# Set-up, first preparation, gate and residual of a masked-attention and ternary-FFN kernel rearranged

## What is computed

```python
norm  = |xn|;  mean = mean of xn over the tokens
score = 0.7 * norm + 0.3 * (-(xn . mean) / (norm * |mean| + 1e-6))
lm    = the int(0.33 * 1024) tokens with the highest score   # landmarks
lm    = lm dilated twice by one token to both sides
mask  = (j <= i) & ((i - j < 128) | lm[j])
s     = softmax(q k^T / 4 + mask) v @ Wo          # 16 heads of 16, 8 k/v heads
w1q, w2q = sign(w) where |w| >= 0.7 * mean|w|, else 0
g     = silu(gelu(xn @ w1q^T + b1) @ w2q^T + b2)  # exact gelu, 1024 hidden
out   = x + s * g
```

## Time and profile before

| | us |
|---|---|
| median of 3 runs | 701.88 (701.42 to 702.69) |
| the profiled execution | 701.2 |
| its span, first to last instruction | 699.5 |
| set-up, to the last copy on ACT | 32.6 |
| first preparation, to turn 0's first matmul | 94.6 |
| PE busy | 581.8 |
| ACT busy | 459.1 |
| DVE busy | 399.2 |
| POOL busy | 260.1 |

### The profile page before, as it was taken

The page is one execution under the profiler, slowest core; times in us unless marked ns, Lnnn a source line. Parts: engine busy times, 40 slices in busy tenths (PEclk is TensorE's granted clock), DMA queues, the critical chain, the costliest instruction groups (busy, mean ns, idle before and its releaser), DMA issues. The chain is left out here.

```text
span 699.5 us, 10945 instructions
## 1 busy us (share of the span) xinstructions
PE 581.8 (83%) x3725; PEld 298.1 (43%) x3725; DVE 399.2 (57%) x957; ACT 459.1 (66%) x584; POOL 260.1 (37%) x303
## 2 busy tenths in 40 slices
PE   1559559889799979889799879889899899799973
PEld 1447315534353636534353635534353545323512
DVE  2757937848557548848557638948475644411111
ACT  4313747787578755787578756787678767797670
POOL 3313523422533433431533433431543353345431
PEclk9779859999999979999999969999999989899995
DMA  7001153202132252202132242102132233031101
GB/s 233 3 2 47 48 116 84 63 8 74 35 93 56 64 146 70 58 9 75 34 94 57 63 146 72 57 9 78 38 101 54 60 84 95 26 89 59 38 15 48
DMA packets 51227, 45.49 MB, mean 65 GB/s; under 512 B 9056, under 2 KB 45536, under 8 KB 51168
## 3 DMA queue, kind: packets, MB, share of 16 engines
q1 hardware_dynamic: 49040, 42.90, 22.1%
q10 hardware_dynamic: 2128, 1.84, 0.8%
HBM read 11.41 MB, written 4.19 MB: 22 GB/s over the span
## 5 line engine op out<-in xcount | busy, mean ns | idle before, releaser
L1575 ACT ACTIVATE f_probs<-sc_ps,shift 128x1024 f32<-128x1024 f32 (+3 forms) x384 | 332.9, 901 | 132.8 <-PE sc_ps L1475 127.5
L1475 PE MATMUL sc_ps<-f_q_stack,f_k_stack 104*128 104x512 bf16 (+3 forms) x768 | 200.3, 352 | 39.3 <-ACT f_probs L1575 22.5
L1492 PE MATMUL att_ps<-f_probs,f_v_sb 128*32 128x512 f32 (+3 forms) x1536 | 168.8, 514 | 12.2 <-POOL f_probs L1634 10.1
L1627 POOL TENSOR_SCALAR_AFFINE_SELECT f_probs<-f_probs 128x512 f32<-128x512 f32 x128 | 94.7, 741 | 131.2 <-ACT f_probs L1575 130.5
L1475 PEld LDWEIGHTS sc_ps<-f_q_stack,f_k_stack 104*128 104x128 bf16 x768 | 48.9, 100 | 205.4 <-ACT f_probs L1575 124.2
L1634 POOL TENSOR_TENSOR f_probs<-f_probs,f_near 128x512 f32<-128x512 f32 x64 | 75.0, 1172 | 110.7 <-ACT f_probs L1575 110.7
L1413 PE MATMUL aux_ps<-w2T,f_h_hi 128*128 128x256 f32 x256 | 72.5, 316 | 0.0
L1614 POOL TENSOR_TENSOR f_h_lo<-f_hid,f_h_hi 128x512 fp32r<-128x512 f32 x36 | 47.9, 1337 | 54.9 <-DVE f_h_hi L1687 47.1
L1492 PEld LDWEIGHTS att_ps<-f_probs,f_v_sb 128*32 128x32 f32 x1536 | 31.4, 110 | 77.4 <-issue 47.7
L1413 PE MATMUL aux_ps<-w2T,f_h_lo 128*128 128x256 f32 x256 | 63.4, 281 | 0.0
L1403 PE MATMUL aux_ps<-f_xT_hi,w1T 128*128 128x512 f32 x128 | 54.7, 427 | 6.8 <-ACT f_hid L1528 6.6
(11 more groups left out here) (174 smaller groups left out, 756.9 us busy)
## 6 DMA issues: line engine op xcount, KB each, us to landing
f_q_stack<-f_q_parts SPq DMA_DIRECT2D x192, 64.0 KB
f_k_stack<-f_k_parts SPq DMA_DIRECT2D x96, 64.0 KB, 2.6
xn<-in_L_attn_hidden_states SPq DMA_DIRECT2D x4, 1024.0 KB, 6.7
f_attT<-f_att_raw SPq DMA_DIRECT2D x128, 32.0 KB
f_rden_bc<-f_den SPq DMA_DIRECT2D x64, 64.0 KB
s_w_nat<-in_L_ffn_w SPq DMA_DIRECT2D x2, 1024.0 KB, 9.1
out_y<-xn SPq DMA_DIRECT2D x4, 512.0 KB, 3.2
xn<-in_L_attn_hidden_states SPq DMA_DIRECT2D x3, 512.0 KB, 3.9
```

The costliest lines, as they stand in the source:

```text
L1475: last = pe.matmul(sc_ps[:, 2 * u + hh, lo:CH], k_stack[0:KROWS + T, h // REP, kb * P:(kb + 1) * P], q_stack[0:KROWS + T, SLOT[n], 2 * u + ...
L1492: last = pe.matmul(att_ps[32 * q:32 * q + 32, n % 2, lo:CH], v_sb[:, kb, j * VW:j * VW + 32], probs[:, i % NPROB, q, lo:CH], start=(kb == ...
L1575: act.activation(probs[:, i % NPROB, us, lo:CH], sc_ps[:, us, lo:CH], ACT.Exp, bias=shift[:, 0:1], scale=HD ** -0.5).then_inc(exp_done, 1)
L1627: pool.affine_select(out=block_probs, in_=block_probs, compare_op=ALU.is_ge, fill=0.0, base=0, pattern=[[0, NQ], [1, P]], channel_multipli ...
```

## The change

1. Set-up. x is the first transfer on SP's queue, and ACT waits for it before it issues the four weight transfers. DVE finishes `rstd` and normalises x before the thresholds. PE sums the normalised x over the tokens (8 matmuls) behind the Gram matmuls; DVE copies the mean row and takes the eight token dots between links of the bound chain.
2. First preparation. Mean row, normalising and token dots are gone from it. Its jobs use six banks (two of `aux_ps`, four of `sc_ps`). The token scores come first on DVE, ranks are laid between the splits of k and q, which use `attT` for their rest, and the wait for the last q split is gone.
3. `rank(t)` takes three instructions: one counts `>=` over the earlier tokens, one `>` over its own and the later ones, one adds the equal ones of its own block that stand ahead.
4. The sum of x over the tokens in a turn is three additions of halves in place of one reduction.
5. silu(z) = z (1 + tanh(z/2)) / 2. ACT takes tanh at steps 15 and 44 between exponentials; DVE multiplies at steps C1 + 3 and 46; the factor 0.5 goes into the product of the output projection. `gates()` is gone.
6. The residual x has a tile `x_res` of its own, filled from step group 0 on, before `att_group(0)`.
7. POOL does the masks of a step before its jobs.
8. `fast_path()` stands in the `If` and `general_path()` in the `Else`.

```diff
@@ set_up @@
+                        sp.dma_start(xn[:, :, :], x[0].rearrange("(t p) d -> p t d", p=P)).then_inc(x_in, 16)
                         sp.dma_start(w1_nat[:, :, :], w1.rearrange("(t p) d -> p t d", p=P)).then_inc(w1_in, 16)
...
-                        act.dma_start(xn[:, :, :], x[0].rearrange("(t p) d -> p t d", p=P)).then_inc(x_in, 16)
+                        act.wait_ge(x_in, 16)
                         act.dma_start(w_nat[:, :, 0:D], Wq.rearrange("(k p) n -> p k n", p=P)).then_inc(wqkv_in, 16)
...
                             layer_norm(dve, lk, k)
+                        for _ in inverse_deviation(dve, lk):
+                            pass
+                        for k in range(T):
+                            dve.tensor_scalar(xn[:, k, :], xn[:, k, :], mv[:, k, 0:1], rstd[:, k:k + 1], ALU.subtract, ALU.mult).then_inc(x_normal, 1)
...
+                        def token_dots(t):
+                            for k in range(t, t + 2):
+                                dve.scalar_tensor_tensor(w_tmp[:, 0, (k - t) * D:(k - t + 1) * D], xn[:, k, :], 1.0, mean_row[:, :],
+                                                         ALU.mult, ALU.mult, accum_out=dots[:, k:k + 1]).then_inc(set_dots, 1)
+                            dve.wait_ge(set_dots, t + 2)
...
+                        dve.wait_ge(mean_sum_done, 1)
+                        dve.tensor_scalar(mean_row[:, :], att_ps[:, 0, 0:D], 1.0 / S, None, ALU.mult).then_inc(mean_out, 1)
...
+                        for t in range(T):
+                            pe.wait_ge(x_normal, t + 1)
+                            last = pe.matmul(att_ps[:, 0, 0:D], ones[:, :], xn[:, t, :], start=(t == 0), stop=(t == T - 1))
@@ fast_path, turn: jobs and banks @@
+                        if main:
+                            jobs += [(s, "mean_row")]
-                        jobs += [(s1 + 17, "score_row", i) for i in range(2)]
-                        jobs += [(s1 + 28, "dilate"), (s1 + 29, "far_rows")]
+                        jobs += [(s1 + 17 if main else 4.4, "score_row", i) for i in range(2)]
+                        jobs += [(s1 + 28, "dilate"), (s1 + 29, "far_rows")] if main else [(18.4, "dilate"), (18.4, "far_rows")]
+                    n_banks = 2 if main else 6
+                    def bank_ps(bank):
+                        return aux_ps[:, bank, :] if bank < 2 else sc_ps[:, bank - 2, :]
-                        return j, (att_raw if j % 2 else resid)[:, :], part
+                        return j, attT[:, j % 2, :], part
@@ SP @@
+                                sp.dma_start(x_res[:, :, :], xb[:, 0:TC, :]).then_inc(xres_in, 16)
+                                if not prep:
+                                    sp.dma_start(xn[:, TC:T, :], xb[:, TC:T, :]).then_inc(xres_in, 16)
                                 att_group(0)
...
-                                    sp.wait_ge(aux_done, n_transposes[-1] + 1)
-                                    sp.wait_ge(dots_done, T)
-                                sp.dma_start(xn[:, 0:x_end, :], xb[:, 0:x_end, :]).then_inc(xres_in, 16)
@@ ACT @@
-                            def gates(c):
+                            def half_tanhs(c):
                                 act.wait_ge(z_done, TC * (c + 1))
-                                act.activation(gate[:, :, :], gate[:, :, :], ACT.Silu).then_inc(gate_done, 1)
+                                if c:
+                                    act.wait_ge(gate_done, c)
+                                act.activation(half_tanh[:, :, :], gate[:, :, :], ACT.Tanh, scale=0.5).then_inc(tanh_done, 1)
@@ POOL @@
-                                    for _, kind, *a in jobs_at(i - 0.5, i + 0.5):
-                                        job(kind, *a)
                                     if i < NSTEP and has_tri(i):
                                         causal(i)
                                     if C1 <= i < NSTEP and has_local(i):
                                         local(i)
+                                    for _, kind, *a in jobs_at(i - 0.5, i + 0.5):
+                                        job(kind, *a)
@@ DVE @@
-                                    dve.tensor_tensor(gate[:, t % TC, :], ps[:, 0:D], gate[:, t % TC, :], ALU.mult).then_inc(prod_done, 1)
+                                    dve.scalar_tensor_tensor(gate[:, t % TC, :], ps[:, 0:D], 0.5, gate[:, t % TC, :], ALU.mult, ALU.mult).then_inc(prod_done, 1)
...
-                                    if not main:
-                                        dve.wait_ge(q_split, QT * NC)
...
-                                lk(dve.scalar_tensor_tensor(junk[:, at], score_row[:, at], own, before[:, :], ALU.is_ge, ALU.mult,
+                                lk(dve.scalar_tensor_tensor(junk[:, at], score_row[:, at], own, before[:, :], ALU.is_equal, ALU.mult,
                                                             accum_out=count[:, t, 2:3]))
-                                lk(dve.scalar_tensor_tensor(junk[:, at], score_row[:, at], own, after[:, :], ALU.is_gt, ALU.mult,
-                                                            accum_out=count[:, t, 3:4]))
...
+                                dve.scalar_tensor_tensor(gate[:, :, :], half_tanh[:, :, :], 1.0, gate[:, :, :], ALU.add, ALU.mult).then_inc(gate_done, 1)
...
-                                        dve.tensor_reduce(xsum[:, :], xn[:, :, :].rearrange("p t d -> p d t"), AX_X, ALU.add).then_inc(xsum_done, 1)
+                                        lk(dve.tensor_tensor(half_sum[:, :, :], xn[:, 0:TC, :], xn[:, TC:T, :], ALU.add))
@@ kernel_program @@
-        with nc.If(exact != 0):
+        with nc.If(exact == 0):
+            fast_path()
+        with nc.Else():
             general_path()
-        with nc.Else():
-            fast_path()
```

103 lines of the change are left out of this document (59 added, 44 removed).

## The result

The changed kernel took 668.97 us (median of 4 runs, 668.27 to 669.42) against 701.65 us for the kernel before on the same chip (699.28 to 702.69): a ratio of 0.954, with a 95% interval of 0.951 to 0.956. The forecast was 665.6 in a range of 654 to 682. The profiled execution took 668.7, its span is 666.9.

A forecast was written before the change was run, and what follows sets the result against it. No engine is full, so time hangs on places where all wait for one. Terms -0.7 - 15.0 + 2.5 - 14.3 + 3.2 - 13.0 + 1.0 = -36.3 take 701.2 to 664.9, median 665.6 us; range 654 to 682.

The forecast's parts named there:

- Set-up and first preparation: From program start to turn 0's first matmul: set-up 0.7 us and preparation 15.0 us less, turn 0 starting at 78.9.
- Step C1: Behind the gelus of each turn: silu, one table load and a shorter reduction save time, clock stays full; -14.3 us.
- Second tanh: At step 44 of each turn, where ACT is nearly full: 0.8 us a turn added, +3.2 us.
- x tile and masks: POOL in the turns: with x early and masks ahead of additions, POOL never holds a mask for either; -13.0 us.
- x_res ahead of att_group(0): Turn 0's queue: the half-megabyte x transfer stands before attention rows due next; +1.0 us.
- The end: End of the program: the jump past the general path is made there instead of at the start; +2.5 us.
- waits for masks under 1 us in all: Sign of being right: PE's values matmuls in the turns wait for POOL's masks under 1 us in all.
- the first (another engine is next in the turns): Rival: turns pay less, another engine being next at the waits removed; 679.8 us, chance 0.2.
- The second: Rival: the start pays less, DVE starting late for another cause and ranks paying contention; 673 us, chance 0.15.
- The third: Rival: more is gained, no charge for end and tanh, preparation at +39; 657.7 us or less, chance 0.15.
- The fourth: Rival: tanh forces table loads of its own, two for each of eight uses; 686 us, chance 0.02.
- The fifth: Rival: slower than before, the denser program keeping PE at the lower clock; 703 us and above, chance 0.02.

## Why the prediction was right, and where its terms were off

The direction, the size and the range held: 32.7 us gained where 36 were forecast. But the sum came this close with errors on both sides: 5.7 us too much for the x tile and the masks and 2.8 of losses left out on the one, 1.5, 2.2 and 0.7 too little for the preparation, step C1 and the second tanh on the other. That they nearly cancel is luck. By its own steps:

- Set-up and first preparation, -15.7 forecast, -17.2 measured. The mechanism held: two chains that meet at the far rows, DVE as early as POOL. Two errors stand against each other in it. The preparation starts 3.0 us earlier than forecast (33.9 for 36.9), since the weights' issue took 2.0 us and not 4.3, x came 0.9 sooner, and mean row and dots put 0.6 on the set-up's second part and not 1.5. And it takes 43.4 us in place of 42, since the fills begin at +20.0 and not at +18. They begin at +17.9 even with no rank ahead of them (the experiment with the ranks behind the splits), and three ranks stand ahead of them where the sum counted two. The contention that the ranks' last operations paid, 4.6 us before, is paid once, 0.9. Taken apart, and counted from each run's own start of the preparation, the interleaving is worth 5.3 and the six banks 6.5; they are not to be added, since either undone leaves the dilation late.
- Step C1, -14.3 forecast, -16.5 measured (steps 14 to 20: 4.3, 4.3, 4.2, 3.7), the tanh included. The tanh cost its whole 1.0 and not 0.7. Turn 3 gave 3.7 in place of 1.7, since the clock was full behind its wait of 1.66 in this trace; seven of the other traces lose about 2 us against it at steps 17 to 20 of turn 3, so it isn't so in each run, and these 2 us are luck of the profiled execution.
- Second tanh, +3.2 forecast, +2.5 measured (0.5, 0.5, 0.5, 1.0). PE does wait for exponentials behind it, 0.37 us in turns 0 to 2 and 1.15 in turn 3.
- x tile and masks, -13.0 forecast, -7.3 measured (steps 20 to 34: 3.5, 2.0, 1.1, 0.7). This is the term that failed. The step "POOL never holds a mask for either" was wrong: an addition that waits for the gate still holds up the masks of the next step. The sum left 0.5 for late masks, and 6.2 us of such waits stay: 3 of 0.99 behind the late addition, 3 of 0.82 behind the product for the gate, which the change itself brought in, and one of 0.78 at the end of turn 3, which the kernel before has too (0.79). In steps 20 to 34 the waits fell from 9.3 to 3.0 us and no low clock follows them; the exponentials gained less than these two added up as the sum had them. And the earlier x has no part in it: the order of the masks alone makes it. How much it makes depends on the kernel around it, 8 us in the kernel before and 11 in the changed one.
- x_res ahead of att_group(0), +1.0 forecast. At steps 0 to 14 of turn 0 nothing is lost. What was lost elsewhere, 3.8 us at the turns' ends (0.7, 0.7, 0.9) and first steps (0.8 and 0.9 in turns 2 and 3, less 0.3 gained in turn 1), was not in the sum: the blocked mask and stretches at the lower clock, such as 384 to 388 in turn 2:

```profile
384.00:388.00 4.00, 4.00 (x16) 1.58 (x15) 1.39 (x5) 2.33 (x3) 0.64 (x1) 0.59 0.59 191
```

- The end, +2.5 forecast, +2.5 measured, by two errors that cancel: the tail behind POOL's last addition is 3.5 longer, of which the branch is the cause, and the last output projection is 1.0 shorter, which the sum did not have.

Of the signs that were to show the prediction wrong one came, the fills' start at +20.0, later than the 18 named, and one in part, PE's waits for ACT behind the tanh at step 44. One of the signs of being right, waits for masks under 1 us in all, did not come (6.2). So the time is right and the mechanism only in part.

Of the rivals the first (another engine is next in the turns) came partly true, at one of its two places, though what is next there is POOL again and not another engine. The second fell: DVE starts 1.1 behind the set-up, and the ranks pay 0.9 for contention. The third fell: the end and the tanh have their prices, and the preparation took 43.4. The fourth fell: there are 18 table loads in place of 26, none for a tanh. The fifth, lower clock by denser work, fell: the mean went from 0.92 to 0.95. The kernel with the x tile late and the jobs first ran once in 670.04 and once in 681.17 with the same instructions. That the spread is the clock's is likely (its granted means were 0.944 and 0.930), but why one execution keeps it up and the other doesn't was not settled. Nor were the ranks with three operations and the reordered set-up tried by themselves.

## What to carry to other kernels

Before giving a late operand a tile of its own, ask what stands behind the waiting instruction in its queue: putting the urgent work (masks that PE waits for) ahead of the patient work (additions to the output) brought 8 us with a few lines swapped, the earlier operand nothing. A wait of PE costs more than its length when the clock falls behind it, as it did behind most of the long waits shown here but not behind all, so read the clock of the microseconds that follow. A new operation on DVE with two operands in SBUF is priced with what POOL does beside it, and its place is looked for where both engines are idle.

## What the runs showed of the chip

- A branch past a large part of the program took PE 3.68 us, at the end of the changed kernel and at the start of the fast path in the kernel before, and cost DVE 3.9 at the start (5.0 less 1.1), while POOL began 0.9 to 1.8 behind the set-up's last copy in both orders.
- A DMA issue of a weight on ACT took 0.44 to 0.49 us behind the landing of x, and 0.53 to 1.84 when all five transfers stood at the program's start.
- The copy of a 128x128 mask on DVE took 0.24 us alone and up to 1.30 in the first preparation and 1.33 in the turns', beside POOL's subtraction:

```profile
L1704 DVE TENSOR_SCALAR f_near<-before,f_landmark x28: 240/243/1328, 70.8 to 520.4; 128x128 bf16<-128x128 bf16 x28
```
